# A cross-attention and expert layer on one core: the choice of experts, a table load, the last routers and two low parts placed anew

## The reference, cut to what matters

```
def smooth_quant_linear(x, w):          # int8 linear with smoothing
    s  = sqrt(max|x| over tokens / max|w| over outputs)      # per column
    xs, ws = x / s, w * s
    x_scale, w_scale = row maxima of |xs|, |ws| / 127
    return round(xs / x_scale) @ round(ws / w_scale).T * x_scale * w_scale.T

x = x + expert_forward(layernorm(x), fside, ctx)    # for each batch: gate/up product, silu, down product

h = layernorm(x)                                    # 2048 tokens
router_logits = h @ gate_w.T                        # 8 experts
sel = top_k(router_logits.sum(over all tokens), 2)  # two experts for all tokens
rw  = softmax(router_logits[:, sel])
x   = x + sum over the two of rw * (gelu(h @ w1[sel] + b1[sel]) @ w2[sel] + b2[sel])
```

## Time and profile before

| | us |
|---|---|
| median of three runs | 821.19 |
| the profiled execution's own time | 820.71 |
| its span, first to last instruction | 818.8 |
| PE busy | 770.2 (94%) |
| DVE busy | 477.9 (58%) |
| POOL busy | 450.6 (55%) |
| ACT busy | 354.6 (43%) |

### The profile page before, as it was taken

The page is one execution under the profiler, slowest core; times in us unless marked ns, Lnnn a source line. Parts: engine busy times, 40 slices in busy tenths (PEclk is TensorE's granted clock), DMA queues, the critical chain, the costliest instruction groups (busy, mean ns, idle before and its releaser), DMA issues.

```text
span 818.8 us, 11350 instructions
## 1 busy us (share of the span) xinstructions
PE 770.2 (94%) x3577; PEld 622.1 (76%) x3577; DVE 477.9 (58%) x669; ACT 354.6 (43%) x660; POOL 450.6 (55%) x497
## 2 busy tenths in 40 slices
PE   5698666899999999999999999999999999999998
PEld 4666454588788888888888888888888888888886
DVE  5999759697754545454545454545454545454545
ACT  3967588643443434343434343434343434342422
POOL 1789997157564646464646464646464646464622
PEclk9899969999999999999999999999999999999999
DMA  9400000401010101010101010101010000000022
GB/s 346 172 2 1 1 0 2 129 1 51 1 52 1 52 0 48 3 46 6 45 7 46 5 46 6 42 9 40 11 39 13 35 16 34 17 34 18 0 103 103
DMA packets 19077, 32.34 MB, mean 39 GB/s; under 512 B 872, under 2 KB 11240, under 8 KB 18160
## 3 DMA queue, kind: packets, MB, share of 16 engines
q1 hardware_dynamic: 18896, 31.98, 11.2%
q10 hardware_dynamic: 160, 0.08, 0.0%
HBM read 27.87 MB, written 4.19 MB: 39 GB/s over the span
## 4 chain that ended last, share of the span: by engine, by line
PE 81%; POOL 8%; DVE 4%; issue 3%; ACT 2%; DMA 1%; ACTq 0%; POOLq 0%; DVEq 0%
PE slot L805 42%; PE slot L792 34%; PE slot L850 3%; POOL wv L366 2%; POOL xf L383 1%; POOL wv L372 1%; PE slot L585 1%; POOL cv L366 1%; DVE rmax L1226 1%; DMA b_rows<-in_L_ffn_b 1%; POOL rstd L340 1%; POOL h_lo L476 1%; DVE stats L1217 1%; DVE peak_x L1226 1%; PE slot L635 1%
## 5 line engine op out<-in xcount | busy, mean ns | idle before, releaser
L792 PE MATMUL slot<-xo,a_hi 128*128 128x512 f32 x840 | 258.9, 389 | 0.0
L1541 DVE SCALAR_TENSOR_TENSOR res<-slot,rw,res 128x512 f32<-128x512 f32 x256 | 178.4, 750 | 130.3 <-PE slot L805 130.2
L1570 DVE TENSOR_TENSOR e<-slot,e 128x512 f32<-128x512 f32 x150 | 103.8, 692 | 173.4 <-PE slot L792 173.3
L805 PE MATMUL slot<-w_hi,h_hi 128*128 128x512 f32 x512 | 201.0, 392 | 0.4 <-POOL h_lo L476 0.4
L805 PE MATMUL slot<-w_lo,h_hi 128*128 128x512 f32 x512 | 199.4, 389 | 0.0
L805 PE MATMUL slot<-w_hi,h_lo 128*128 128x512 f32 x512 | 199.3, 389 | 0.0
L792 PEld LDWEIGHTS slot<-xo,a_hi 128*128 128x128 f32 x840 | 157.3, 188 | 33.4 <-DVE e L1570 0.2
L476 POOL TENSOR_TENSOR h_lo<-e,h_hi 128x512 fp32r<-128x512 f32 x96 | 138.2, 1454 | 55.1 <-ACT e L1104 54.1
L792 PE MATMUL slot<-xo,a_lo 128*128 128x512 f32 x420 | 163.4, 389 | 0.0
L805 PEld LDWEIGHTS slot<-w_hi,h_hi 128*128 128x128 f32 x512 | 96.1, 188 | 25.1 <-POOL h_lo L476 5.6
L476 POOL TENSOR_TENSOR h_lo<-hid,h_hi 128x512 fp32r<-128x512 f32 x32 | 44.1, 1379 | 124.1 <-ACT hid L1104 124.1
(11 more groups left out here) (145 smaller groups left out, 812.3 us busy)
## 6 DMA issues: line engine op xcount, KB each, us to landing
raw<-in_L_ffn_w SPq DMA_DIRECT2D x32, 512.0 KB, 3.4
res<-in_x SPq DMA_DIRECT2D x4, 1024.0 KB, 11.9
wv<-in_fside_BxS2xS SPq DMA_DIRECT2D x4, 1024.0 KB, 13.0
out_x<-res SPq DMA_DIRECT2D x3, 1024.0 KB, 3.9
cv<-in_ctx SPq DMA_DIRECT2D x4, 512.0 KB, 13.5
out_x<-res SPq DMA_DIRECT2D x4, 256.0 KB, 2.7
b_row<-in_L_ffn_b SPq DMA_DIRECT2D x2, 256.0 KB, 4.4
b_rows<-in_L_ffn_b ACTq DMA_DIRECT2D x1, 64.0 KB, 5.8
```

What stands on the lines that cost most here:

```text
L792: last = t.matmul(dst, a[:, i, k, :], xo[tp][:, v, k, :], start=(start and n == 0), stop=(n == 3 * H - 1), skip_group_check=True)
L805: last = t.matmul(y_bank[j][:, :], a[:, i, j * P:(j + 1) * P], v[:, f, :], start=(start and n == 0), stop=(not start and n == 2), skip_gro ...
L1541: v.scalar_tensor_tensor(out=r, in0=y_bank[j][:, :], scalar=rw[:, ds(p, 1), n:n + 1].rearrange("p a b -> p (a b)"), in1=r, op0=ALU.mult, o ...
L1570: v.tensor_tensor(dst[:, :], src, other[:, :], ALU.add).then_inc(comb_ready, 1)
```

## The change

Five edits, all in the stretch between the second layer norm and the first pair of weight blocks:

1. In the slots, router 2 goes from slot 1 to slot 3 (behind e), so that router 3 stands right behind y.3.1 in slot 1.
2. POOL gets a function `keep_lo`, and makes both low parts of batch 0 behind `inv_std(3, 2)`, its last operation of the stage. DVE makes them no more.
3. On ACT the table load (`gelu_warm`) goes from between two high parts to behind the weights' high parts, the logits of batch 0 are copied before those of batch 1, and those of batches 2 and 3 behind the table load, ahead of the down weights.
4. On DVE `choose_experts` stands right behind `token_total`, with both low parts of batch 2 behind it.
5. On DVE `pick_experts` and `pick_bias` stand behind the low parts of the weights.

```diff
@@ SLOT_USES
-             "a.2 s2.0 p2.0.1 y.3.1 r.2 r.3 "),
+             "a.2 s2.0 p2.0.1 y.3.1 r.3 "),
...
-             "p1.2.0 r2.0 wq1.3.0 r2.1 xq2.0 a.3 wq2.1 wq2.2 p2.2.0 s2.3 p2.3.1 y.1.0 y.2.1 e "),
+             "p1.2.0 r2.0 wq1.3.0 r2.1 xq2.0 a.3 wq2.1 wq2.2 p2.2.0 s2.3 p2.3.1 y.1.0 y.2.1 e r.2 "),
@@ POOL
+            def keep_lo(b, h):
+                pool.wait_ge(hi_ready[b], h + 1)
+                tp, p = b // 2, b % 2
+                g.tensor_tensor(whole(tp, LO_AT[p][h]), part(tp, FULL_AT[p][h]),
+                                whole(tp, HI_AT[p][h]).bitcast(F32), ALU.subtract).then_inc(lo_ready[b], 1)
...
             inv_std(3, 2)
+            keep_lo(0, 0)
+            keep_lo(0, 1)
@@ ACT
             keep_hi(2, 0)
-            s.activation(gelu_warm[:, :], half[:, 0:1], ACT.Gelu_apprx_tanh)
             keep_hi(2, 1)
             keep_summed(3, 1)
             keep_hi(3, 0)
             keep_hi(3, 1)
+            keep_logits(0)
             keep_logits(1)
-            keep_logits(2)
-            keep_logits(0)
             first_weights(0, 2)
             first_weights(2, 4)
+            s.activation(gelu_warm[:, :], half[:, 0:1], ACT.Gelu_apprx_tanh)
+            keep_logits(2)
+            keep_logits(3)
             first_down_weights()
-            keep_logits(3)
@@ DVE
             moments(3, 2)
-            keep_lo(0, 0)
             keep_lo(1, 0)
             normalise_last()
             token_sums(2)
             keep_lo(1, 1)
             token_sums(3)
             token_total()
-            keep_lo(0, 1)
+            choose_experts()
             keep_lo(2, 0)
-            choose_experts()
             keep_lo(2, 1)
-            pick_experts()
             keep_lo(3, 0)
             keep_lo(3, 1)
-            pick_bias()
             first_weights(0, 2)
             first_weights(2, 4)
+            pick_experts()
+            pick_bias()
             first_down_weights()
             pick_logits()
```

## The result

The changed kernel takes 823.04 us in the median (822.06 to 825.44, 22 runs) against 821.33 (820.65 to 823.74, 22 runs) for the kernel before: a ratio of 1.0024, 95% interval 1.0017 to 1.0031. It is slower, by 0.24%, and by 1.7 us between the medians. The forecast was 820.3, 0.9 us faster; the time lies in the range, on the other side of no change.

A forecast was written before the change was run, and what follows sets the result against it. PE bounds the expert layer, its first matmul held by DVE's low parts; with picks and table load moved and POOL's hold counted, that matmul came at 152.7 instead of 153.61, 0.9 us earlier: 821.19 to 820.3 us, range 818.6 to 823.1.

The forecast's parts named there:

- What bounds the kernel: Expert layer runs at PE's pace (busy 660.83 of 665.19 us); a change ahead is worth what it moves the first expert matmul.
- the worth of the other edits: Ahead of the first expert matmul: picks free 1.5 and 0.51 us on DVE, table load 1.28 us on ACT; choice costs 0.63.
- The inverse root gained nothing: POOL's last inverse root: losing DVE's second subtraction of batch 0 could gain 0 to 0.5 us; taken as 0.
- ended before 138: Sign that the forecast is wrong: POOL's last inverse root ending before 138 us.
- Whether POOL is in DVE's way: At the end of stage 1: both engines exclude each other while working on SBUF, normalise_last included; said to decide the sum.
- double rate: DVE's normalise_last: 0.5 us per 512-column operation, read as twice one stream's speed, so taken to use both paths.
- no harm: POOL leaves normalise_last alone: first expert matmul 1.85 us earlier, 819.3 us (818.8 with a sooner inverse root); chance 0.22.
- POOL starved: POOL's second low part waits through DVE's four low parts: first expert matmul 5.2 us later, 826.4 us; chance 0.05.
- The sum, DVE first: Up to the first expert matmul: normalise_last precedes POOL, batch 1's low part 1.2 us late; 0.9 us faster, 820.3; chance 0.42.
- normalise_last 139.0 to 140.0: First step of the sum, on DVE: normalise_last runs unheld in 1.0 us, POOL's first low part after it.
- POOL first: POOL's first low part holds normalise_last to 142.25, its second batch 1's part: 1.3 us slower, 822.5 us; chance 0.28.
- The order itself: Whether DVE's normalise_last or POOL's first low part gets hold first: 0.42 for DVE, 0.28 for POOL.

The follow-up runs named there:

- e10: Kernel of e1 with the one-hot and bias rows picked ahead of the weights' low parts again, as before the change: 821.91 us, ratio 1.0000.
- e7: Kernel of e1 with the choice of experts back behind a low part of batch 2: 820.12 us, ratio 0.9985.
- e11: Kernel of e1 with the table load back between the two high parts of batch 2: 820.31 us, ratio 0.9984.
- e12: Kernel of e1 with routers 2 and 3 both in slot 1 and batch 2's logits copied ahead of the weights: 820.30 us, ratio 0.9980.
- e9: Kernel of e1 with eighteen transposes added in PE's idle time ahead of batch 2: 819.10 us, ratio 0.9974.
- e3: Kernel before with one part of the change alone, both low parts of batch 0 on POOL: 824.56 us, ratio 1.0035.
- e4: Changed kernel with each of POOL's two 1024-column subtractions issued as two of 512: 819.97 us, ratio 0.9988.
- e5: Changed kernel with twelve more transposes on PE while it waits for the second half of normalise_last: 822.40 us, ratio 1.0008.
- e2: Changed kernel with POOL waiting for the end of normalise_last before its two subtractions: 819.14 us, ratio 0.9976.
- e6: Changed kernel with all four tiles of batch 3 normalised by ACT and normalise_last gone: 820.39 us, ratio 0.9982.
- e8: Kernel of e2 with eighteen transposes added in PE's idle time ahead of batch 2: 819.57 us, ratio 0.9969.
- e1: Changed kernel with both low parts of batch 0 back on DVE, all other moves kept: 819.60 us, ratio 0.9980.

## Why the prediction was wrong

*What bounds the kernel, and the worth of the other edits: right.* The first expert matmul decides, and all after it moved as a block: behind it PE waited 0.4 us once, before and after alike. The picks (e10) are worth the most, the choice's place possibly something (e7), the table load and the slots nothing that the times can tell (e11, e12), though the profiles of e9 and e11 give the table load about 1.1 us. No gelu behind the table load held PE. The inverse root gained nothing, as taken: its product ended 2.87 us after DVE's last moments operation (L1231, 134.91 + 0.18) against 2.91 before. That it ended before 138, a sign I had named, came from the earlier end of stage 1 in this profile.

*Whether POOL is in DVE's way: right in kind.* normalise_last does contend with POOL, as its double rate suggested; the rival "no harm" falls. So does "POOL starved": both subtractions were done by 142.74.

*"The sum, DVE first", its first step "normalise_last 139.0 to 140.0": this step failed.* It took 5.04 us instead of 1.00, since POOL got hold first, in all four profiles in which its subtraction stood free behind the inverse root's product (changed, e3, e4, e5). Put in its place by hand (e2), the rest of the sum held: batch 1's subtraction ended 4.57 us after the inverse root's product instead of 3.31 before, 1.26 us late (1.2 forecast), and the kernel was faster than before, by 0.24% (0.1% forecast; the token total came 5.84 us after the inverse root's product instead of the 5.9 of the sum, and the four low parts took 4.61 us instead of 4.75).

*The rival "POOL first" was the right mechanism, but too small.* It had 1.3 us and the profile shows 2.24. I let both operations of normalise_last go one after the other once POOL's first subtraction had ended. In fact they took turns with POOL: one behind its first, one behind its second, to an end 5.07 us after the inverse root's product (143.03 - 137.96) where the rival had 3.3. The subtraction of batch 1 was then not held any more (1.21 us), which gave 1.1 of it back. And it had no term for the clock, which cost 0.7 (e5). That 823.04 still lies inside the range, 0.06 us below its end, is luck in part: the end is this rival's 822.5 and half a microsecond more. The alternation could have been read off the lines behind the earlier trace rows:

```profile
184.88 2.27 POOL L476 TENSOR_TENSOR h_lo<-e,h_hi 128x512 fp32r<-128x512 f32 x1
186.04 2.20 DVE L1310 TENSOR_TENSOR xf<-xf 128x1024 f32<-128x1024 f32 x1
```

After 184.92 DVE's held operation ran, to 186.00, and POOL's next waited for it (2.27 us instead of 1.3), and DVE's next for that one (2.20 instead of 1.2). I let batch 1's subtraction be held a second time in this way and not normalise_last. The turns are not strict, though: POOL's operation at 181.16 waited through three subtractions of DVE before it ran, from about 183.7. Why it got no turn between these is open.

*The order itself I had at 0.42 to 0.28 for DVE.* POOL's operation starts 0.08 us before DVE's (137.91 and 137.99), and 0.08 or 0.09 in e3, e4 and e5. That such a lead is not always enough is seen in the same timelines: POOL's last tile of batch 2 started at 134.90, DVE's subtraction at 135.01, and it was DVE that went through (1.22 us) and POOL that took 1.81 instead of 0.8. In the kernel before it was the other way about, with starts at 135.91 and 136.06. For this pair the other profiles agree: with a lead of POOL of 0.07 to 0.11 us DVE went first, with 0.14 to 0.17 POOL. Why 0.08 us suffice against normalise_last stays open. Its two per-partition scalars need not be the reason: in e6 POOL's second low part led a subtraction of DVE, which has none, by 0.11 us (141.34 and 141.45) and went first too, though there it stood right behind another of POOL's own.

## What to carry to other kernels

Before moving an elementwise operation from VectorE to GpSimd, look at what VectorE runs beside it in the new place. While both work on SBUF, each operation of one can be held for a whole operation of the other: here two of 0.5 us took 2.56 us each beside GpSimd operations of 2.35. So short operations on a critical path suffer most, and long ones on GpSimd do most harm. Let GpSimd wait until the critical ones are through (e2), or cut its operations (e4). ScalarE did such work beside GpSimd at its usual 0.73 us a tile (e6).

Where an operation releases another engine and its own engine's next operation starts within a tenth of a microsecond of the released one, don't count on either order: price both, and if one is bad, write the order down.

## What the runs showed that I had not expected

The granted clock followed PE's own idle time in this stage: after 3.4 us without work ahead of batch 2 it had a mean of 0.50 to 0.72 from 134 to 140 us in the profiles without added transposes there (0.54 in e2, 0.72 before), and with eighteen idle transposes there 1.00 throughout (e8, e9). A wait of 2.04 us in the changed kernel was followed by 0.50 from 144 to 147 us, and with transposes in it by 1.00 (e5). Idle time alone does not settle it: with waits of 0.81 and 0.94 us ahead of batch 3, the clock from 140 to 144 us was 0.50 in e1 and 1.00 before. But in the changed kernel a hold on another engine was paid twice, once as the wait and once as the slower matmuls behind it.
